# Attention with a gated feed-forward network: three of four chunks of the probabilities turned in blocks instead of two

## The reference

```python
theta_x = einsum('ld,bdt->btl', theta_w, context) + theta_b
phi_x   = einsum('ld,bdt->blt', phi_w, layernorm(x)) + phi_b[:, None]
p       = softmax(einsum('btl,bls->bts', theta_x, phi_x), axis=-1)
g_x     = einsum('ld,bdt->btl', g_w, layernorm(x)) + g_b
t_x     = einsum('bts,bsl->blt', p, g_x)
h       = relu(layernorm over a whole batch of t_x * ln_gamma + ln_beta)
x       = x + tanh(g0) * (einsum('ol,blt->bot', out_w, h) + out_b + context)
# second half: y = quant(rmsnorm(layernorm(x)))
x       = x + tanh(g1) * bitlinear(silu(bitlinear(y, w1)) * bitlinear(y, w2), w3)
```

## Time and profile before

| what | value |
|---|---|
| median of three runs | 298.15 us (298.07 to 298.43) |
| the profiled execution | 298.3 us |
| its span | 296.5 us |
| TensorE busy | 291.0 us, 98% of the span |
| VectorE busy | 239.8 us, 81% |
| ScalarE busy | 195.5 us, 66% |
| GpSimd busy | 197.8 us, 67% |
| chain that ended last, by engine | TensorE 79%, VectorE 6%, GpSimd 4% |
| TensorE's granted clock | 1.0 of full speed in all stages read |

### The profile page before, as it was taken

The page is one execution under the profiler, slowest core; times in us unless marked ns, Lnnn a source line. Parts: engine busy times, 40 slices in busy tenths (PEclk is TensorE's granted clock), DMA queues, the critical chain, the costliest instruction groups (busy, mean ns, idle before and its releaser), DMA issues.

```text
span 296.5 us, 4393 instructions
## 1 busy us (share of the span) xinstructions
PE 291.0 (98%) x1310; PEld 155.6 (52%) x1310; DVE 239.8 (81%) x539; ACT 195.5 (66%) x319; POOL 197.8 (67%) x302
## 2 busy tenths in 40 slices
PE   8999999999999999999999999999999999999996
PEld 5665757575757565644444444444444444444444
DVE  3797888989898786999889787986986896867872
ACT  2388888989898898799765645465456456345620
POOL 3353598959593958657798777786786786655710
DMA  7999587858594001010335374334343362651355
GB/s 261 414 416 410 200 277 292 282 153 330 167 343 143 0 2 35 1 39 0 71 71 62 87 140 106 63 81 106 72 97 83 76 107 68 131 116 29 83 100 180
DMA packets 56535, 42.23 MB, mean 142 GB/s; under 512 B 43456, under 2 KB 46656, under 8 KB 55488
## 3 DMA queue, kind: packets, MB, share of 16 engines
q1 hardware_dynamic: 56224, 41.69, 48.8%
q10 hardware_dynamic: 288, 0.27, 0.3%
HBM read 24.65 MB, written 6.82 MB: 106 GB/s over the span
## 4 chain that ended last, share of the span: by engine, by line
PE 79%; DVE 6%; POOL 4%; issue 3%; DMA 3%; ACT 2%; SPq 1%; POOLq 0%; DVEq 0%
PE bank L1238 37%; PE bank L1256 14%; PE bank L1182 8%; PE bank L1154 5%; PE bank L1199 4%; PE bank L1118 3%; PE bank L1169 3%; PE bank L1131 2%; DMA x<-x_dram 2%; PE bank L1141 2%; POOL stage L401 2%; PE bank L1269 1%; DMA probT<-prob 1%; POOL prob L385 1%; DVE blocks L772 1%
## 5 line engine op out<-in xcount | busy, mean ns | idle before, releaser
L1238 PE MATMUL bank<-wq,stage 128*128 128x512 bf16 x512 | 113.3, 379 | 0.0
L1238 PEld LDWEIGHTS bank<-wq,stage 128*128 128x128 bf16 x512 | 50.1, 98 | 61.6 <-issue 2.3
L872 DVE SCALAR_TENSOR_TENSOR stage<-bank,s,stage 128x512 f32<-128x512 f32 x64 | 47.6, 744 | 22.6 <-PE bank L1238 18.6
L615 ACT ACTIVATE xn<-stage 128x1024 f32<-128x1024 f32 x31 | 32.8, 1057 | 46.0 <-DVE stage L872 46.0
L607 ACT ACTIVATE stage<-bank,s 128x512 f32<-128x512 f32 x64 | 43.1, 680 | 16.5 <-PE bank L1238 14.4
L1256 PE MATMUL bank<-wq,prob 128*128 128x512 bf16 x224 | 50.5, 379 | 0.0
L467 POOL TENSOR_SCALAR stage<-stage,hsc 128x1024 f32<-128x1024 f32 x30 | 33.3, 1119 | 20.6 <-DVE hsc L903 20.6
L877 DVE TENSOR_REDUCE m<-stage 128x1 f32<-128x1024 f32 x31 | 37.7, 1216 | 0.8
L1256 PEld LDWEIGHTS bank<-wq,prob 128*128 128x128 bf16 x224 | 21.9, 98 | 26.5
L1154 PE MATMUL bank<-ph,th 128*128 128x512 f32 x96 | 34.4, 471 | 0.2 <-DVE ph L753 0.2
L473 POOL TENSOR_SCALAR prob<-stage 128x1024 bf16<-128x1024 f32 x30 | 30.9, 1044 | 0.0
(11 more groups left out here) (122 smaller groups left out, 460.4 us busy)
## 6 DMA issues: line engine op xcount, KB each, us to landing
stage<-w1t_dram SPq DMA_DIRECT2D x4, 1024.0 KB, 11.7
stage<-w2t_dram SPq DMA_DIRECT2D x4, 1024.0 KB, 8.5
stage<-w3t_dram SPq DMA_DIRECT2D x4, 1024.0 KB, 6.7
x<-x_dram SPq DMA_DIRECT2D x7, 512.0 KB, 8.4
c_sb<-ctx_in_dram SPq DMA_DIRECT2D x7, 512.0 KB, 7.2
out_dram<-stage SPq DMA_DIRECT2D x14, 256.0 KB, 2.4
spill<-blocks SPq DMA_DIRECT2D x5, 512.0 KB, 2.6
placed<-spill SPq DMA_DIRECT2D x20, 128.0 KB, 2.8
```

Of the source, the lines that this page charges most:

```text
L615: A.activation(junk, h_sb[t % 2][:, half * HF:(half + 1) * HF], ACT.Square, accum_out=ssq[:, half:half + 1]).then_inc(sq_done, 1)
L872: V.scalar_tensor_tensor(h_sb[k][:, c * 512:(c + 1) * 512], up_banks(n)[1][:, :], s12[:, u % 2, 1, k:k + 1], sil[n % 3], ALU.mult, ALU.mul ...
L1238: last = mm(bank[:, :], turned[:, row:row + P], wq[:, at:at + 512], start=q == 0, stop=q == KI - 1)
```

## The change

Batches 2 to 5 now take the way by blocks for chunks 1, 2 and 3, and TensorE turns only chunk 0. Batch 1 stays as it was. `first_block(i)` gives the first chunk that goes by blocks (2 for batch 1, 1 for batches 2 to 5, else 4), and the counts of the semaphores are made from it. The tiles `blocks` and `placed` and the scratch tensor grow from 8 chunks' worth of columns to 12. A batch's transfer out is 768 KB and each of its four transfers back 192 KB. `values(i, 1)` of these batches moves one stage later, in front of `values(i, 2)`. On ScalarE one copy of a turned chunk falls away for each of these batches. Apart from that, the third weight's quarter 2 is issued directly behind its quarter 1, ahead of `move_blocks(4)` instead of behind it.

```diff
-        blocks = sb("blocks", [P, TC * 2 * P])
-        placed = sb("placed", [P, 4, 2 * P])
-        spill = nc.dram_tensor("spill", [P, TC * 2 * P], F32, kind="Internal").ap()
+        blocks = sb("blocks", [P, TC * 3 * P])
+        placed = sb("placed", [P, TC * 3 * P])
+        spill = nc.dram_tensor("spill", [P, TC * 3 * P], F32, kind="Internal").ap()
...
+        def first_block(i):
+
+            return 2 if i == 1 else 1 if 2 <= i <= B - 3 else TC
+
         def by_blocks(i):
 
-            return 1 <= i <= B - 3
+            return first_block(i) < TC
...
             def move_blocks(i):
 
-                sp.wait_ge(blocks_ready, 2 * i)
+                n = TC - first_block(i)
+                sp.wait_ge(blocks_ready, block_no(i))
                 if i >= 2:
                     sp.wait_ge(blocks_moved, 64 * (i - 1))
-                sp.dma_start(spill[:, :], blocks[:, :]).then_inc(blocks_out, 16)
+                sp.dma_start(spill[:, 0:TC * n * P], blocks[:, 0:TC * n * P]).then_inc(blocks_out, 16)
                 sp.wait_ge(blocks_out, 16 * i)
                 sp.wait_ge(tx_done, i)
                 for k in range(4):
-                    sp.dma_start(placed[32 * k:32 * (k + 1)], spill_v[k]).then_inc(blocks_moved, 16)
+                    back = spill[:, k * n * P:(k + 1) * n * P].rearrange("(q b) r -> b q r", b=32)
+                    sp.dma_start(placed[32 * k:32 * (k + 1), 0:TC * n * P].rearrange("b (q r) -> b q r", q=4), back)\
+                        .then_inc(blocks_moved, 16)
...
             load_weight(2, 1)
+            load_weight(2, 2)
             move_blocks(4)
-            load_weight(2, 2)
             load_c(7)
...
                 if i >= 1:
-                    p_copy(i - 1, 0)
-                    p_copy(i - 1, 1)
+                    for c in range(min(first_block(i - 1), 2)):
+                        p_copy(i - 1, c)
...
-                if by_blocks(i - 1):
-                    turn_blocks(i - 1, 0)
-                    turn_blocks(i - 1, 1)
+                for c in range(first_block(i - 1), TC):
+                    turn_blocks(i - 1, c)
...
-                if by_blocks(i - 2):
-                    values(i - 2, 2)
-                    values(i - 2, 3)
+                if i >= 2:
+                    for c in range(first_block(i - 2), TC):
+                        values(i - 2, c)
...
-                if i >= 1:
+                if i >= 1 and first_block(i - 1) > 1:
                     turn_p(i - 1, 1)
...
-                elif i >= 1:
+                elif i >= 1 and first_block(i - 1) > 1:
                     values(i - 1, 1)
```

More of the change, by code:

```diff
@@ L78, in gated_cross_attention_bitffn @@
         probT = sb("probT", [P, 2, T])
-        blocks = sb("blocks", [P, TC * 2 * P])
-        placed = sb("placed", [P, 4, 2 * P])
-        spill = nc.dram_tensor("spill", [P, TC * 2 * P], F32, kind="Internal").ap()
-        spill_v = spill.rearrange("(q b) (k r) -> k b q r", b=32, k=4)
+        blocks = sb("blocks", [P, TC * 3 * P])
+        placed = sb("placed", [P, TC * 3 * P])
+        spill = nc.dram_tensor("spill", [P, TC * 3 * P], F32, kind="Internal").ap()
         hn = sb("hn", [P, T])
@@ L153, in b_turn, with block_no @@
             return banks[2] if (i, c) == (B - 1, 2) else banks[4] if i == B - 1 and c == 3 else b_pt[c % 2]
+        def first_block(i):
+            return 2 if i == 1 else 1 if 2 <= i <= B - 3 else TC
         def by_blocks(i):
-            return 1 <= i <= B - 3
+            return first_block(i) < TC
         def turn_no(i, c):
-            return c + (2 * i + 2 if by_blocks(i) else 0 if i == 0 else 2 * (B - 3) + 4 * (i - (B - 3)))
+            return c + sum(first_block(j) for j in range(i))
+        def block_no(i):
+            return sum(TC - first_block(j) for j in range(i + 1))
         def turned_p(i, c):
-            if by_blocks(i) and c >= 2:
-                return placed[:, :, (c - 2) * P:(c - 1) * P].rearrange("s q (c r) -> s q c r", c=TC)
+            if c >= first_block(i):
+                n = TC - first_block(i)
+                return placed[:, 0:TC * n * P].rearrange("s (q k c r) -> s k q c r", q=4, k=n, c=TC)[:, c - first_block(i)]
             return c_sb[:, 0, 0] if (i, c) == (B - 1, 2) else probT[:, 0] if i == B - 1 and c == 3 else probT[:, c % 2]
@@ L764, in sum_inverse, with turn_blocks @@
                 V.reciprocal(rsum[:, :], esum[:, :]).then_inc(rsum_ready, 1)
-            def turn_blocks(i, k):
-                if k == 0:
+            def turn_blocks(i, c):
+                n = TC - first_block(i)
+                if c == first_block(i):
                     dve.wait_ge(pnorm_ready, 4 * i + 4)
@@ L771, in turn_blocks @@
                         dve.wait_ge(blocks_out, 16 * (i - 1))
-                V.transpose(blocks[:, :].rearrange("p (s k c r) -> p k c s r", s=4, k=2, c=TC)[:, k],
-                            prob[:, i % 2, :, (2 + k) * P:(3 + k) * P].rearrange("p c (s r) -> p c s r", r=32))\
+                V.transpose(blocks[:, 0:TC * n * P].rearrange("p (s k c r) -> p k c s r", s=4, k=n, c=TC)[:, c - first_block(i)],
+                            prob[:, i % 2, :, c * P:(c + 1) * P].rearrange("p c (s r) -> p c s r", r=32))\
                     .then_inc(blocks_ready, 1)
@@ L944, in third_step @@
                 low_part(2, th, b_th, 0, th_ready, thl_ready)
-                turn_blocks(1, 0)
-                turn_blocks(1, 1)
+                for c in range(first_block(1), TC):
+                    turn_blocks(1, c)
                 low_part(2, ph, b_ph, 1, ph_ready, phl_ready)
```

## The result

The changed kernel takes 301.75 us (median of 4 runs, 300.98 to 303.55) against 298.23 (298.07 to 298.43) before on the same chip: a ratio of 1.0128 [1.0109, 1.0148], slower, outside the range of the prediction. Its profiled execution took 300.98 us, with a span of 299.2, 2.7 us over the profiled execution of before; it is the fastest of the four.

The account below looks back on a forecast made before the run. It took TensorE to bound the kernel, with VectorE close behind. VectorE's -0.68 at batch 6's first product became about -0.65 with transfers: 298.3 - 0.65 = 297.65, or 297.5 us against the median; range 296.6 to 298.8.

Parts of the forecast that it names:

- The weight's quarter issued earlier counts nothing: Loads ahead of batch 4's write: quarters 1 and 2, 2 MB, take 7.1 us, to 75.3, so no cost.
- Rival 3: Batch 2's transfers: both legs stretch with their bytes, a wait of 3.8, +3.0 us, 301.2; chance 0.09.
- Rival 2: Batch 2 lands late in stage 4: TensorE waits 0.8 to 1.44, giving 298.2 to 298.85; chance 0.27.
- The walk: VectorE's delay followed through stages 3 to 7, 0.65 added per transposition: +0.26 in stage 4, -0.68 in stage 7.
- The gate: First product of batch 6, in stage 7, waiting for VectorE: predicted to move by -0.68, to near 108.8.
- Rival 1: TensorE's own sum holds as VectorE catches up: 296.4, or 297.05 with stage 3's 0.65; chance 0.18.
- The forecast's own parts: Gate in stage 7 moves -0.68 by VectorE; batch 2's expected wait of 0.1 makes that about -0.65.
- The fourth rival: VectorE absorbs nothing: each batch costs it 0.65 and gives TensorE 0.44, +0.84, 299.0; chance 0.06.

Follow-up runs that it names:

- e1: The changed kernel with the third weight's quarter 2 put back behind batch 4's transfers: 299.76 us (1.0054).
- e2: The kernel before, two chunks, with only the third weight's quarter 2 issued early, ahead of batch 4's transfers: 298.08 us (0.9986).
- e7: The changed kernel with three unread filler multiplications on TensorE ahead of batch 4's block products: 299.76 us (1.0065).
- e3: The changed kernel with six unread filler multiplications on TensorE ahead of batch 4's block products: 301.48 us (1.0104).
- e5: The changed kernel, early quarter kept, with only two of three chunks transferred; the third product reads the first chunk's place: 296.69 us (0.9955).
- e6: e1 with the third weight's quarter 3 directly behind quarter 2, ahead of batch 7's context load: 298.34 us (1.001).
- e11: e6 with the scatter made on writing: four writes of 192 KB and one read of 768 KB per batch: 297.28 us (0.9962).
- e12: e11 with the change's own load order, quarter 2 ahead of batch 4's transfers, quarter 3 behind batch 7's context load: 298.04 us (0.9989).
- e9: Three chunks, e6's load order, blocks sent straight to placed in sixteen transfers per batch without DRAM: 303.69 us (1.0203).

## Why the prediction was wrong

**The step that failed** is the last paragraph of its section on transfers: "The weight's quarter issued earlier counts nothing ... the 2 MB of both take 7.1 us, to 75.3, just when the write of batch 4 is issued". The sum left out what stood in the queue ahead of those 2 MB. At 68.07 these were the reads of batch 3, the first quarter (issued at 66.06) and context 6 (67.64), 2.36 MB less the 0.66 moved by 68: 1.70 MB. With the same 296 GB/s the sum gives (1.70 + 2.10) / 0.296 = 12.8 us, to 81, and all bytes of the write after that. The kernel before issues the same loads at 63.03, 64.82 and 67.73, so its trace had what the sum needed. The prediction reckoned batch 4's last read at 84.2 "needed at 85.8"; it came at 87.93, needed at 87.97 - 2.35 = 85.62. e1 shows the step from the other side (quarter back: the write lands after 3.3, no wait), and e2 that the same order costs nothing where all transfers are as before.

**What it did not foresee at all** is that a wait is paid twice. Every rival priced a wait at its length; a wait of 2.35 us cost 4.0, the other 1.7 at 1.2 GHz (e7). Rival 3 had a figure near the truth, 301.2, but by luck: it put a wait of 3.8 at batch 2 and stretched both legs in proportion to their bytes. The Trainium skill, "TensorE: Matmul & The Clock Gate", section HAM oscillation, says that products behind a wait for a DMA can start at 1.2 GHz and that half of the throttled time is lost. The trace agrees on the price: the mean granted clock over the 4.37 us was 0.61, and the missing 0.39 of 4.37 is 1.70 us. It does not agree on the start: the first half microsecond behind the wait still ran at 0.93.

**Right, by their numbers.** Stage 3: the mean product was predicted at 49.5 and `theta(4)` at 54.04; they came at 49.13 and 53.70, with `theta(3)` 0.31 earlier than before, so 49.44 and 54.01 on the old scale. Batch 2: the first block product was predicted near 57.7 with little wait; 57.39, 57.70 on that scale, and no wait (its write landed at 51.4, where the prediction had 51.55). `theta(6)`: 82.22 predicted, 82.02, or 82.33 on that scale. Three of VectorE's transpositions take 1.90 us against 1.30 for two, so the third costs 0.60 where the prediction had 0.65. TensorE and VectorE by time, stages 3 to 5:

```profile
49.13 0.38 PE L1216 MATMUL bank<-tsc,avg 128*128 128x1 f32 x2 [0.69 <-DVE tsc L794]
...
57.39 1.98 PE L1193 MATMUL bank<-placed,gs 128*128 128x512 f32 x4
```

```profile
59.06 1.90 DVE L784 STREAM_TRANSPOSE blocks<-prob 128x512 f32<-128x512 f32 x3 [0.38 <-ACT prob L600]
...
63.89 0.22 DVE L799 TENSOR_SCALAR tsc<-bank,tsc 128x1 f32<-128x1 f32 x1 [0.26 <-PE bank L1216]
...
77.87 0.22 DVE L799 TENSOR_SCALAR tsc<-bank,tsc 128x1 f32<-128x1 f32 x1 [0.31 <-PE bank L1216]
```

Rival 2, batch 2 late, did not happen in this execution, but it is not out: e3 and e7 show waits of 0.84 and 1.35 us at that place, which is the size that the rival had (0.8 to 1.44). It came on top of the loss in stage 6 and does not explain it.

**Too pessimistic on VectorE**, the second step that failed. Its waits ahead of `tx_dev` were to vanish; 0.26 and 0.31 of them are left, of 0.84 and 0.93. The walk kept the delay of stage 4 as a lasting one, but the 0.38 us ahead of the transpositions, which it had used up, is still there (59.06, above), and TensorE's list sets the period: 13.98 us in stage 5, busy for all of it. The gate was said to move with VectorE, by -0.68, behind a TensorE wait of about 1 us. The wait is 0.55, as before, because `tst`, which opens VectorE's chain to the gate, itself waits for a product of TensorE (0.26):

```profile
106.75 0.70 DVE L790 BATCH_NORM_STATS2 tst<-bank 128x6 f32<-128x512 f32 x1 [0.26 <-PE bank L1193]
```

So the gate moves with TensorE. Rival 1 had this, between 296.4 and 297.05 (chance 0.18), and e5's 296.69 shows it for the engines' side. The forecast's own parts were -0.68 for the engines and +0.03 for the transfers; the runs give -1.47 and +5.06. The fourth rival, VectorE absorbing nothing (299.0), is out by the same run.

**A late weight.** The prediction put the question and then closed it ("if the quarter 1 came late, ScalarE's sums of magnitudes would, and their cover is ScalarE's free time"). It was the last quarter that came late. ScalarE by time, stage 6 of the changed kernel:

```profile
92.23 1.91 ACT L544 ACTIVATE wq<-stage 128x2048 bf16<-128x2048 f32 x1 [2.51 <-DMA stage<-w3t_dram]
```

This wait lies beneath TensorE's own delay; in e1 and e6 it comes to the surface as 0.9. What stays open is why executions of the changed kernel lie between 300.98 and 303.55 where before's lie within 0.4: only the fastest was profiled. The waits at batch 2 in e3 and e7 are one candidate, worth up to 1.35, and the start of stage 3, which varies by 1.5 us, another; neither was tested.

## What to carry over

Sum the queue before pricing a transfer: every byte issued since the DMA share was last well below 1, in order, divided by the rate in that stretch, and only then the landing time of an idle queue. Before moving a load earlier, look for the small transfer behind it that another engine waits for, and reckon that the products behind a wait of TensorE can run at 1.2 GHz: here a wait of 2.35 us cost 1.7 more, while waits of 1.35 and 1.62 us left the clock at 1.00. Where a transfer's chain is write, wait, read, put the many pieces and the many issues on the write's side, in front of the wait: behind the landing they are paid in full (e11, e12).

## What the runs showed of the hardware

- A wait of 2.35 us was followed by a granted clock of 0.50, from half a microsecond after TensorE was at work again until past 91.5; waits of 1.35 (e7, stage 4) and 1.62 us (e9, stage 3) left the clock at 1.00.
- The DMA engines can be full at 240 to 250 GB/s (66 to 70 us, with the reads in 1.5 KB pieces in it) and at 390 to 430 (74 to 80, weights and the write).
- The same 768 KB write landed 3.3 (batch 3, when the reads were issued) to 6.9 us (batch 4) after its issue, by what stood ahead of it; in e1 batch 4's too landed after 3.3. The Trainium skill, "DMA: Bandwidth & Descriptors", section Latency and other measured facts, gives 0.2 us on average and 2 us at high load for the access to HBM; the 3.6 us between these landings are twice what that allows for, and e1 and the sum of bytes lay them to the queue.
- Sixteen transfers of 48 KB between two SBUF tiles kept SyncE for 10.0 us, 0.63 each, against 0.44 for each of four reads of 192 KB from DRAM.
